# AdaLN with a mixture of experts on one core: the head's residual sum moved from VectorE to TensorE, the first norm spread over three engines

## What is computed

```python
mod = (silu(c) @ wmod).reshape(2, 6, 1, 128)      # sa, ca, ga, sb, cb, gb for each sequence
ga = sign(ga) * max(|ga|, 0.25); gb likewise
h = layernorm(x) * (1 + ca) + sa
x = x + ga * running_mean(h)                      # mean over the tokens up to this one
h = layernorm(x) * (1 + cb) + sb
x = x + gb * (experts(h) + shared(h))
```

## Time and profile before

| | us |
|---|---|
| median of 3 runs (lowest to highest) | 380.26 (378.79 to 380.68) |
| the profiled execution | 376.93 |
| its span, first to last instruction | 375.1 |
| granted TensorE clock over the span | 0.902 |
| VectorE's first bit count starts | 65.94 |
| GpSimd's first gather starts | 115.12 |

### The profile page before, as it was taken

The page is one execution under the profiler, slowest core; times in us unless marked ns, Lnnn a source line. Parts: engine busy times, 40 slices in busy tenths (PEclk is TensorE's granted clock), DMA queues, the critical chain, the costliest instruction groups (busy, mean ns, idle before and its releaser), DMA issues.

```text
span 375.1 us, 4615 instructions
## 1 busy us (share of the span) xinstructions
PE 282.0 (75%) x1020; PEld 145.4 (39%) x1020; DVE 169.8 (45%) x798; ACT 136.0 (36%) x224; POOL 210.7 (56%) x218
## 2 busy tenths in 40 slices
PE   0768979899998676879899889889969757975000
PEld 0646757243344333444444434444433323332000
DVE  1899993577787374463444444444110111011100
ACT  1147776344333132324344433444433222432000
POOL 2355542000005746563788888888888887876660
PEclk9999785599999999989999999999998989899555
DMA  8908301013003575634555555555554453432230
GB/s 228 320 17 227 84 29 30 0 57 42 2 1 114 159 202 143 180 109 122 114 94 105 107 111 107 112 110 112 115 110 84 84 128 72 56 56 27 28 28 7
DMA packets 49884, 35.95 MB, mean 96 GB/s; under 512 B 7815, under 2 KB 44478, under 8 KB 49854
## 3 DMA queue, kind: packets, MB, share of 16 engines
q0 software_dynamic: 13824, 14.46, 22.8%
q1 hardware_dynamic: 35792, 20.73, 20.0%
q10 hardware_dynamic: 238, 0.42, 0.5%
HBM read 23.65 MB, written 11.94 MB: 95 GB/s over the span
## 4 chain that ended last, share of the span: by engine, by line
POOL 41%; issue 22%; PE 13%; DMA 3%; DVE 2%; POOLq 1%
POOL out_dram L844 26%; POOL R L831 15%; PE U L962 5%; PE Y L987 4%; DMA out_dram<-YO,IDXB 3%; PE LG L993 1%; PE Y L916 1%; PE R L867 1%; DVE R L463 0%; POOLq L201 0%; POOL RS L796 0%; DVE GJ L695 0%; PE R L1026 0%; DVE TK L622 0%; DVE TK L599 0%
## 5 line engine op out<-in xcount | busy, mean ns | idle before, releaser
L844 POOL DMA_INDIRECT out_dram<-YO,IDXB x72 | 113.5, 1577 | 34.6 <-issue 21.5
L831 POOL DMA_INDIRECT R<-rows_scratch,IDXB x72 | 70.0, 972 | 88.6 <-DVE IDXB L712 67.7
L365 ACT ACTIVATE HF<-U,CB 128x512 f32<-128x512 f32 x72 | 49.4, 687 | 78.3 <-PE U L968 60.5
L968 PE MATMUL U<-XT,XW 128*128 128x512 f32 x144 | 76.5, 613 | 0.7 <-issue 0.7
L987 PE MATMUL Y<-HF,XW 128*128 128x512 f32 x144 | 76.6, 617 | 0.0
L746 DVE SCALAR_TENSOR_TENSOR YO<-R1b,GT,R 128x128 f32<-128x128 f32 x72 | 20.3, 344 | 91.3 <-PE R1b L867 84.2
L365 ACT ACTIVATE HF<-U,COL 128x512 f32<-128x512 f32 x32 | 22.0, 688 | 49.0 <-PE U L962 34.1
L987 PEld LDWEIGHTS Y<-HF,XW 128*128 128x128 f32 x144 | 27.6, 198 | 30.8 <-issue 30.8
L962 PE MATMUL U<-H2F,WS 128*128 128x512 f32 x64 | 37.9, 679 | 0.0
L968 PEld LDWEIGHTS U<-XT,XW 128*128 128x128 f32 x144 | 26.5, 196 | 26.6 <-issue 26.5
L987 PE MATMUL Y<-HF,WS 128*128 128x512 f32 x64 | 35.6, 639 | 0.0
(11 more groups left out here) (144 smaller groups left out, 342.5 us busy)
## 6 DMA issues: line engine op xcount, KB each, us to landing
XW<-in_L_ffn_W_dram SPq DMA_DIRECT2D x36, 256.0 KB
XW<-in_L_attn_x_dram SPq DMA_DIRECT2D x8, 256.0 KB, 7.0
rows_scratch<-GBC SPq DMA_DIRECT2D x2, 1024.0 KB, 7.9
rows_scratch<-HT SPq DMA_DIRECT2D x8, 256.0 KB, 2.4
out_dram<-SHO SPq DMA_DIRECT2D x8, 256.0 KB
R<-rows_scratch,IDXB POOLq DMA_INDIRECT x72
out_dram<-YO,IDXB POOLq DMA_INDIRECT x72
INV<-in_inv_dram SPq DMA_DIRECT2D x4, 256.0 KB, 6.2
```

Source lines behind the costliest of these rows:

```text
L365: eng.activation(HF[:, g % RING, :], UB[g % 2][:, :], ACT.Gelu_apprx_tanh, bias=bias).then_inc(M["a_gelu"], 1)
L831: eng.indirect_dma_start(XG[:, v % XR, s, :], None, rows_dram, bass.IndirectOffsetOnAxis(ap=IDXB[:, v, s:s + 1], axis=0)).then_inc(M[f"ld_ ...
L844: eng.indirect_dma_start(out, bass.IndirectOffsetOnAxis(ap=IDXB[:, v, s:s + 1], axis=0), YO[:, v % 2, s, :], None, compute_op=ALU.add).the ...
L968: eng.matmul(bank[:, :], WU[:, v % WR, c * P:(c + 1) * P], XT[:, v % 2, :], start=True, stop=True).then_inc(M["pe_up"], 1)
```

## The change

- `prefix` is one scan now: CT[t] = CT[t-1] * t/(t+1) + XN[t]/(t+1), which gives the running mean itself. INV is turned into the ratio t/(t+1) = 1 - 1/(t+1) in four pieces of 512: the first by VectorE before the loop, the others by ScalarE (`ratio(1..3)`), each behind `keep_x2(0..2)`.
- The factor 1/(t+1) goes into the first norm's scale: GpSimd multiplies by `INVT`, a copy of 1/(t+1) with tokens on partitions, which comes with ROWS by a seventh small load and a transpose.
- x is not transposed any more. TensorE adds in PSUM, in token order: x (through the identity), the shift (a matmul of ones with a diagonal matrix `DCB`), and the running means (CT transposed and scaled by one matmul with a diagonal `DCA` for each tile). `add_x` has the first two, `add_means` the third. The diagonals are made by VectorE (`diagonals`). The sum stands in `YB`, double-buffered, where it stood in RB[0].
- `norm1`: ScalarE tile 0, GpSimd tile 1, VectorE tiles 2 and 3.
- The last block: statistics and norm are taken by VectorE straight from its bank, ahead of the softmax of the first part; `keep_x2(7)` comes late. GpSimd leaves two small steps of its `rstd2(7)` out.
- ScalarE touches Exp once before `norm2(6)`, so that the table is loaded there.

```diff
-                for t in range(2):
-                    m = eng.activation(XN[:, b % 2, t, :], X[:, b, t, :], ACT.Identity,
-                                       bias=RS[:, 0, b, 1, t:t + 1], scale=RS[:, 0, b, 0, t:t + 1])
-                m.then_inc(M["a_xn"], 1)
+                eng.activation(XN[:, b % 2, 0, :], X[:, b, 0, :], ACT.Identity, bias=RS[:, 0, b, 1, 0:1],
+                               scale=RS[:, 0, b, 0, 0:1]).then_inc(M["a_xn"], 1)
+
+            def ratio(q):
+                eng.wait_ge(M["ld_inv"], 16 * NT)
+                eng.activation(INV[:, q, :], INV[:, q, :], ACT.Identity, bias=ONES[:, 0:1],
+                               scale=-1.0).then_inc(M["a_rat"], 1)
...
                 if j < NB - 1:
                     keep_x2(j)
+                if j + 1 < NT:
+                    ratio(j + 1)
+
+            eng.wait_ge(M["g_half"], 1)
+            eng.activation(EXPT, NHALF[:, 0:1], ACT.Exp)
             norm2(NB - 2)
+            expo(0)
             affine2(NB - 2)
             affine2(NB - 1)
-            expo(0)
+            keep_x2(NB - 1)
             expo(1)
...
+                if b % 4:
+                    eng.wait_ge(M["a_rat"], b % 4)
...
                 if b >= 2:
                     eng.wait_ge(M["pe_t3"], b - 1)
-                eng.scalar_tensor_tensor(ACC[:, b % 2, :], T2[:, :], CB[:, n:n + 1], MT, ALU.add,
-                                         ALU.add).then_inc(M["v_x2"], 1)
+                eng.tensor_tensor_scan(CT[:, b % 2, :], INV[:, b % 4, :], UB[b % 2][:, :], init, ALU.mult,
+                                       ALU.add).then_inc(M["v_ct"], 1)
...
+            def diagonals(n):
+                eng.wait_ge(M["v_mod"], 9)
+                eng.wait_ge(M["ld_cst"], 16)
+                eng.tensor_scalar(DCB[:, n, :], IDENT, CB[:, n:n + 1], None, ALU.mult).then_inc(M["v_dg"], 1)
+                eng.tensor_scalar(DCA[:, n, :], IDENT, CA[:, n:n + 1], None, ALU.mult).then_inc(M["v_dg"], 1)
...
+            diagonals(0)
+            eng.wait_ge(M["ld_inv"], 16 * NT)
+            eng.tensor_scalar(INV[:, 0, :], INV[:, 0, :], -1.0, 1.0, ALU.mult, ALU.add).then_inc(M["v_rat"], 1)
+            eng.wait_ge(M["v_rat"], 1)
...
+                eng.tensor_tensor(PW[:, b, :], VE[:, 0, b, :], NHALF, ALU.pow).then_inc(M["g_pw1"], 1)
+                eng.wait_ge(M["g_pw1"], b + 1)
+                eng.wait_ge(M["v_cols"], 1)
+                eng.tensor_tensor(RS[:, 0, b, 0, :], PW[:, b, :], INVT[:, NT * (b % 4):NT * (b % 4) + NT],
+                                  ALU.mult).then_inc(M["g_sc1"], 1)
...
+            rstd1(0)
+            norm1(0)
+            rstd1(1)
+            norm1(1)
...
-            rstd(0, 2)
-            for j in range(NB + 1):
+            rstd1(2)
+            for j in range(NB):
+                if 1 <= j < NB - 1:
+                    norm1(j + 1)
                 if j:
-                    rstd(1, j - 1)
+                    rstd2(j - 1)
                 if j + 3 < NB:
-                    rstd(0, j + 3)
+                    rstd1(j + 3)
+            rstd2(NB - 1)
...
+            def add_x(b):
+
+                n = b // 4
                 if b >= 2:
-                    eng.wait_ge(M["v_x2"], b - 1)
-                transposes(YB[b % 2], lambda t: X[:, b, t, :]).then_inc(M["pe_t2"], 1)
...
+                    eng.wait_ge(M["a_x2"], b - 1)
+                eng.wait_ge(M["v_dg"], 2 * n + 2)
+                eng.matmul(YB[b % 2][:, :], IDENT, X[:, b, :, :].rearrange("p t c -> p (t c)"), start=True, stop=False)
+                eng.matmul(YB[b % 2][:, :].rearrange("p (t c) -> p t c", t=NT), ONES,
+                           DCB[:, n, :].unsqueeze(1).to_broadcast([P, NT, P]), start=False, stop=False)
+
+            def add_means(b):
+                n = b // 4
+                eng.wait_ge(M["v_ct"], b + 1)
+                for t in range(NT):
+                    m = eng.matmul(YB[b % 2][:, t * P:(t + 1) * P], CT[:, b % 2, t * P:(t + 1) * P], DCA[:, n, :],
+                                   start=False, stop=t == NT - 1)
+                m.then_inc(M["pe_t3"], 1)
...
             turn_x(0)
+            add_x(0)
             for j in range(NB):
                 if j + 1 < NB:
                     turn_x(j + 1)
                 if j == NB - 1:
-                    turn_x2(j)
+                    add_means(j)
+                elif j + 1 < NB:
+                    add_x(j + 1)
...
                 if j < NB - 1:
-                    turn_x2(j)
+                    add_means(j)
```

More of the change, by code:

```diff
@@ L116, in adaln_moe @@
         ROWS = sb("ROWS", [P, P])
-        COL = sb("COL", [P, 64])
-        B1, B2, GWC = COL[:, 0:36], COL[:, 36:45], COL[:, 47:55]
+        COL = sb("COL", [P, 55 + SEQ // P])
+        B1, B2, GWC, INVT = COL[:, 0:36], COL[:, 36:45], COL[:, 47:55], COL[:, 55:55 + SEQ // P]
+        DCA, DCB = sb("DCA", [P, 2, P]), sb("DCB", [P, 2, P])
         XW = sb("XW", [P, NB * BLK])
@@ L443, in stats2 @@
             def stats2(b):
-                eng.wait_ge(M["a_x2"], b + 1)
-                stats(1, b, X2[:, b, :].rearrange("p (t c) -> p t c", t=NT), "v_ag2")
+                if b < NB - 1:
+                    eng.wait_ge(M["a_x2"], b + 1)
+                    src = X2[:, b, :]
+                else:
+                    eng.wait_ge(M["pe_t3"], b + 1)
+                    src = YB[b % 2][:, :]
+                stats(1, b, src.rearrange("p (t c) -> p t c", t=NT), "v_ag2")
             def norm1(b):
@@ L514, in softmax @@
                 n = t1 - t0
-                logits = LG[:, 0:n * E] if part == 0 else YB[0][:, 0:n * E]
+                logits = LG[:, 0:n * E] if part == 0 else RB[0][:, 0:n * E]
                 logits = logits.rearrange("p (t e) -> p t e", e=E)
@@ L548, in vector @@
                                           ALU.mult).then_inc(M["v_gbd"], 1)
+                    diagonals(1)
                 if j:
@@ L552, in vector @@
                     stats1(j + 3)
+            stats2(NB - 1)
+            norm2_last()
             softmax(0, 0)
-            stats2(NB - 1)
+            softmax(0, 1)
             eng.memset(EQ0[:, 0:1], 0.0).then_inc(M["v_zero"], 1)
@@ L786, in gpsimd, with rstd1 @@
             used = None
-            def rstd(k, b):
-                q = str(k + 1)
-                eng.wait_ge(M["v_ag" + q], b + 1)
+            def rstd1(b):
+                eng.wait_ge(M["v_ag1"], b + 1)
                 eng.wait_ge(M["g_half"], 1)
[L793 to L799, removed]
@@ L801, in gpsimd @@
-            rstd(0, 0)
-            rstd(0, 1)
+                eng.tensor_scalar(VE[:, 0, b, :], MV[:, 0, b, :, 1], 1.0, EPS, ALU.mult, ALU.add).then_inc(M["g_ve1"], 1)
+                eng.tensor_scalar(NM[:, 0, b, :], MV[:, 0, b, :, 0], -1.0, 0.0, ALU.mult, ALU.add).then_inc(M["g_nm1"], 1)
+                eng.wait_ge(M["g_ve1"], b + 1)
+                eng.tensor_tensor(PW[:, b, :], VE[:, 0, b, :], NHALF, ALU.pow).then_inc(M["g_pw1"], 1)
+                eng.wait_ge(M["g_pw1"], b + 1)
+                eng.wait_ge(M["v_cols"], 1)
@@ new lines, in rstd1, with rstd2 @@
+                eng.tensor_tensor(RS[:, 0, b, 0, :], PW[:, b, :], INVT[:, NT * (b % 4):NT * (b % 4) + NT],
+                                  ALU.mult).then_inc(M["g_sc1"], 1)
+                eng.wait_ge(M["g_sc1"], b + 1)
+                eng.wait_ge(M["g_nm1"], b + 1)
+                eng.tensor_tensor(RS[:, 0, b, 1, :], NM[:, 0, b, :], RS[:, 0, b, 0, :], ALU.mult).then_inc(M["g_rs1"], 1)
+            def rstd2(b):
+                eng.wait_ge(M["v_ag2"], b + 1)
+                eng.tensor_scalar(VE[:, 1, b, :], MV[:, 1, b, :, 1], 1.0, EPS, ALU.mult, ALU.add).then_inc(M["g_ve2"], 1)
+                if b < NB - 1:
+                    eng.tensor_scalar(NM[:, 1, b, :], MV[:, 1, b, :, 0], -1.0, 0.0, ALU.mult,
+                                      ALU.add).then_inc(M["g_nm2"], 1)
+                eng.wait_ge(M["g_ve2"], b + 1)
+                eng.tensor_tensor(RS[:, 1, b, 0, :], VE[:, 1, b, :], NHALF, ALU.pow).then_inc(M["g_pw2"], 1)
+                if b == NB - 1:
+                    return
+                eng.wait_ge(M["g_pw2"], b + 1)
+                eng.wait_ge(M["g_nm2"], b + 1)
+                eng.tensor_tensor(RS[:, 1, b, 1, :], NM[:, 1, b, :], RS[:, 1, b, 0, :], ALU.mult).then_inc(M["g_rs2"], 1)
@@ L803, in gpsimd, with norm1 @@
+            def norm1(b):
+                eng.wait_ge(M["g_rs1"], b + 1)
+                if b >= 2:
+                    eng.wait_ge(M["pe_t1"], b - 1)
+                eng.tensor_scalar(XN[:, b % 2, 1, :], X[:, b, 1, :], MV[:, 0, b, 1, 0:1], RS[:, 0, b, 0, 1:2],
+                                  ALU.subtract, ALU.mult).then_inc(M["g_xn"], 1)
+            rstd1(0)
+            norm1(0)
+            rstd1(1)
+            norm1(1)
             eng.wait_ge(M["ld_cst"], 16)
```

65 lines of the change are left out of this document (21 added, 44 removed).

## The result

The changed kernel took 390.38 us (median of 4 runs, 389.47 to 390.75), the kernel before 380.24 (378.79 to 380.68): a ratio of 1.027, 95% interval 1.0237 to 1.0303. It is slower by 10.1 us, where 7.5 were forecast, inside the stated range. The profiled execution has a span of 388.9 us.

The account below looks back on a forecast made before the run. Bound: one string of head, softmax, bit search, indices and first gather, so the first count's start decides. Between +2.7 and +9.3 us by TensorE's clock, +7.5 was taken: 380.26 + 7.5 = 387.8 us, range 381 to 391.

Parts of the forecast that it names:

- The string: Head, `keep_x2(0)` through ratio, scan, diagonals, stats2, `rstd2`, `rstd1` to GpSimd's block 3 tile: 9.0 us, `turn_x(3)` 5.3 late.
- Blocks 5 to 7: Late head: no ratio or `rstd1` ahead, so TensorE binds; 9.7 us at high clock, about 11.7 with one low stretch.
- `add_means(0)` seen by ScalarE: Start of the head: TensorE's first transposes, `add_x` and means end at 22.0 us, clock rising at about 19.
- from there to `turn_x(3)`: Head, from `keep_x2(0)` through VectorE and GpSimd to block 3's tile: 9.0 us, so `turn_x(3)` starts at 31.0.
- `turn_x(3)` to `turn_x(5)`: Blocks 3 to 5: the waiting loop spans two turns, 12.4 us at high clock, 14.5 with low stretches.
- `keep_x2(6)` to the first count: End of the head: ScalarE sets it, 14.3 us against 14.6 before; the table load takes back most of the gain.
- first count, against before: Start of VectorE's bit search, before at 65.94 us: +9.3 low clock, +5.1 high in the loop, +2.7 high throughout.
- The seventh small load: Start of the head: the extra load of 1/(t+1) is hidden by block 2's statistics and costs nothing.
- The low case of the loop: Blocks 3 to 7 with TensorE's clock low in stretches after idling: first count +9.3 us.
- one sign of being wrong: Bit search shorter than 38 us, which would take back what the head loses.
- The rival that TensorE's work is the bound: Head loop: TensorE's 4.85 us a turn binds whatever the order; in e1 under 2 us gained, no chance given.
- The port: Head: GpSimd's tiles may wait out VectorE's 0.49 us norm, 1.5 us more over three loops by the page.

Follow-up runs that it names:

- e1: Changed kernel with GpSimd making the first-norm tile of block j+2 at the start of turn j, ahead of both `rstd`: 365.83 us, ratio 1.0082 to the kernel before.
- e2: Changed kernel with ScalarE making the three remaining ratios right after block 1's first norm, not behind `keep_x2(0..2)`: 366.76 us, ratio 1.0102 to the kernel before.
- e6: Changed kernel with the shift's float32 matmul made as two float16 matmuls (diagonal and its remainder): 389.27 us, ratio 1.0279 to the kernel before.
- e4: Changed kernel with 1/(t+1) as 16 more columns of the constants, no seventh small load or wider transpose: 372.45 us, ratio 1.0238 to the kernel before.
- e10: e8 with the Exp table loaded right behind Silu, before the head's loop, the other order kept: 376.60 us, ratio 0.9923 to the kernel before.
- e9: e8 with the Exp table load and `expo(0)` put back behind the last `affine2` and `keep_x2(7)`: 375.65 us, ratio 0.9882 to the kernel before.
- e8: e7 with the float16 shift of e6: 375.03 us, ratio 0.993 to the kernel before.
- e7: Changed kernel with the edits of e1, e2 and e4 together: 378.60 us, ratio 1.0006 to the kernel before.
- e5: Changed kernel with unused 512-column TensorE matmuls, six ahead of `turn_x(3)` and two ahead of `turn_x(5)`: 383.90 us, ratio 1.0132 to the kernel before.
- e11: e10 with three unused 512-column TensorE matmuls in its gaps at the end of the head: 374.29 us, ratio 0.9856 to the kernel before.

## Why the prediction was right

*The direction and the mechanism.* The string that was forecast is the one in the rows, link by link, and e1 and e2 show two of its links by taking them out. Blocks 5 to 7 were forecast as bound by TensorE, and e6 agrees. TensorE's idle wait for GpSimd's tile, the low clock behind it and the order in which the later blocks lose came as forecast; the times are below.

*The terms.* Each against what it measured:

| step | forecast | measured |
|---|---|---|
| `add_x(0)` starts | 15.2 | 16.52 |
| `add_means(0)` seen by ScalarE | 22.0 | 24.00 |
| from there to `turn_x(3)` | 9.0 | 9.5 |
| `turn_x(3)` to `turn_x(5)` | 12.4 to 14.5 | 15.4 |
| `turn_x(5)` to `turn_x(7)` | 9.7 to 11.7 | 11.6 |
| `turn_x(7)` to `keep_x2(6)` | 3.7 | 3.7 |
| `keep_x2(6)` to the first count | 14.3 | 14.1 |
| first count, against before | +9.3 (low clock) | +12.4 |

Two sums came out low on paper: the steps up to `add_means(0)` add to 22.25 where I wrote 22.0, and those of the string to 9.4 where I wrote 9.0, since the hand-overs were left out. And three terms were too small. The seventh small load was not hidden in this execution: the transpose of ROWS waits for it until 10.63, and modulation ends at 15.88, not at 14.75. By the spread of the start (e4) much of this can be chance. The clock in the start rose about 2 us later than the 19 that I let it rise at: TensorE's steps take their low-clock times until about 21. And GpSimd's tile takes 0.80 us, not 0.35; the upper bound that I had set from the row with constants, 0.7, was too low as well. It counts in two loops, those that end at `turn_x(3)` and `turn_x(5)`; `turn_x(7)` doesn't wait.

*The choice between the ends.* I took 7.5 out of 2.7 to 9.3, nearer to the low clock. The low case of the loop was right, and its 9.3 with the 3.1 us above gives the 12.4. That the total lies inside the range is in part luck. I had the search at its old length, and by that 12.4 us in the head would have made 392.7, outside the 381 to 391. But the search gave 1.8 us back: about its first microsecond ran at the low clock, in the kernel before its first seven.

*The signs.* `turn_x(3)` waits for GpSimd's tile, TensorE is idle then, the clock is 0.50 after it. The times that I had named with these were missed: `stats2(0)` starts at 27.31 and not near 25, `turn_x(3)` at 33.52 and not at 29 to 32, the first count at 78.35 and not at 70 to 76. And one sign of being wrong is there, a search shorter than 38 us: it takes 36.3.

*The end of the head.* The forecast 14.3 us came out at 14.1, against 14.6 before. That the last block's norm from its bank gives next to nothing fits this, but no run has that edit alone. The reason was incomplete. I named the table load as what takes the gain back. e10 shows that `expo(0)`, waiting for VectorE ahead of `affine2(6)`, holds the same place when the load is gone; e9, which undoes both, is the one that wins 1.2 us to the count over e8, some of it by the clock.

*The rival that TensorE's work is the bound* has its point too. It is wrong for the changed kernel up to `turn_x(5)` (e1, e6) and right as soon as the string is cut (e7, e8): 10 of 10 us busy. A turn is then 5.01 us, where 4.85 were reckoned, so the new head gains a few tenths in each turn behind the first ones. e7 is no faster than the kernel before because it starts 3.1 us late at `turn_x(3)`. The forecast had that late start (`add_means(0)` 2.9 us later) and priced it inside its sum; it measured 4.8 (24.00 against 19.16). No run takes it out.

*The port.* The Trainium skill (Advanced Engine Details and Errata, Mode Summary) says that GpSimd and VectorE's two-port instructions block each other. The tile takes 0.80 us also at 52.57, where VectorE is idle, so its length isn't that. The drain that the Trainium skill (ScalarE: Activation LUTs, What ACT_TABLE_LOAD costs) adds isn't there in this trace either: the load at 67.92 takes 1.28 us and is followed by its activation at 69.22.

*What stays open.* The profile doesn't say how the clock of one execution relates to that of the next, so the split of e1's gain into string and clock rests on one profiled execution each; e5 gives the clock's share by timing, some 5 of the 10 us. Whether e9 is truly faster than e8, or only not slower, the intervals leave open. What the late start costs at the end isn't shown: an order with `turn_x(1)` ahead of `add_x(0)` wasn't tried.

## What to carry to other kernels

Taking work off the busiest engine pays only if its waits don't grow: before moving a small piece to an idle engine, write down what stands ahead of it in that engine's list and what those things wait for. Here the same 0.8 us tile cost 7 us behind two `rstd` and little ahead of them. In this kernel an idle gap of TensorE was paid twice, as the gap and as the low clock behind it, and work that nobody reads was worth its time there (e5, e11). A step that is put ahead of others in an engine's list brings its own waits with it: `add_x(0)` made every later block wait for the diagonals.

## What the runs showed of the hardware

- A 128x128 float32 TENSOR_SCALAR on GpSimd takes 0.80 us with two scalars from memory and 0.30 with constants.
- With seven small loads into ROWS the transpose waited until 9.62 (e1) to 10.63 us (the changed kernel) in six profiled executions, with six until 7.65 (e10) to 8.95 us (before) in eight, though the seventh was issued only 0.3 us behind the sixth.
- One chip ran the kernel before in 362.92 us, the others in 378.4 to 380.2. In e1, on that chip and with the same code in this stage, the stretch from the first gather (117.15) to the first scatter (164.14) is 47.0 us; in the kernel before, on another, it is 61.3 (115.12 to 176.39). VectorE's index steps show 9.5 us of waits there for something outside the five engines, and none in e1. What it was is not settled.
